# Second layer of a two-layer transformer block: another fill order, the maxima rows of half 0 asked for sooner, the last scaling and stores shared out anew

## The reference

```
x = layernorm(x + attention0(x))      # 16 heads of 8, q and k rms-normed
x = layernorm(x + moe(x))             # top-1 router, 16 experts of 128 -> 512 -> 128, capacity 320
x = layernorm(x + attention1(x))      # 16 heads, d_k 8, d_v 64, causal, then Wo (1024 -> 128)
x = layernorm(x + coupling_ffn(x))    # three cycles of: out += coupling(out) * twist(out)
```

## Time and profile before

| what | value |
|---|---|
| time before, median of 3 runs | 821.2 us (820.27 to 821.78) |
| the profiled execution, its own time | 832.08 us |
| its span (first to last instruction) | 830.4 us |
| PE busy | 775.0 us, 93% of the span |
| DVE / ACT / POOL busy | 63% / 56% / 37% |
| mean granted clock of PE | 0.981 of full speed |

### The profile page before, as it was taken

The page is one execution under the profiler, slowest core; times in us unless marked ns, Lnnn a source line. Parts: engine busy times, 40 slices in busy tenths (PEclk is TensorE's granted clock), DMA queues, the critical chain, the costliest instruction groups (busy, mean ns, idle before and its releaser), DMA issues.

```text
span 830.4 us, 19969 instructions
## 1 busy us (share of the span) xinstructions
PE 775.0 (93%) x7472; PEld 442.4 (53%) x7472; DVE 521.8 (63%) x1400; ACT 464.3 (56%) x737; POOL 311.2 (37%) x466
## 2 busy tenths in 40 slices
PE   6899999999989997899999999999999999999992
PEld 4444444444667776455455555555556555556440
DVE  7488888886511113755766667764776666646556
ACT  3798898899322221364544445543554445554675
POOL 5134433443471004343442345432544323224505
PEclk9799999999999999999999999999999999999997
DMA  6344455433166542315542445414553234222003
GB/s 197 84 114 126 130 136 132 116 103 97 39 147 168 165 124 65 89 50 105 110 85 64 78 103 109 101 38 82 109 110 79 63 65 97 59 59 57 2 1 101
DMA packets 111740, 78.08 MB, mean 94 GB/s; under 512 B 12529, under 2 KB 103089, under 8 KB 111649
## 3 DMA queue, kind: packets, MB, share of 16 engines
q1 hardware_dynamic: 105088, 69.85, 35.1%
q0 software_dynamic: 3664, 5.70, 2.8%
q10 hardware_dynamic: 2896, 1.31, 0.6%
HBM read 37.86 MB, written 13.63 MB: 62 GB/s over the span
## 4 chain that ended last, share of the span: by engine, by line
PE 41%; SPq 12%; DVE 7%; DMA 5%; issue 4%; POOL 2%; ACT 1%; DVEq 0%; POOLq 0%
PE l_ps_v L1473 7%; PE l_ps_c L1446 6%; SPq L113 5%; SPq L115 5%; PE ex_ps_h L1067 5%; PE ex_ps_y L1086 4%; PE l_ps_d L1459 3%; DMA q_ring<-l_max_rows 3%; PE l_ps_v L1374 2%; DVE l_rden L2033 2%; PE l_by_query L1395 2%; DVE l_neg_max L2021 1%; PE l_by_key L1573 1%; PE l_by_query L1386 1%; PE l_by_key L1428 1%
## 5 line engine op out<-in xcount | busy, mean ns | idle before, releaser
L2021 DVE TENSOR_REDUCE l_neg_max<-l_by_query 128x6 bf16<-128x768 f32 x125 | 119.6, 957 | 119.1 <-PE l_by_query L1399 118.8
L2303 POOL TENSOR_SCALAR_AFFINE_SELECT l_probs<-l_probs 128x512 f32<-128x512 f32 x128 | 87.2, 681 | 195.6 <-ACT l_probs L1726 194.7
L1726 ACT ACTIVATE l_probs<-l_by_key 128x768 f32<-128x768 f32 x128 | 103.7, 810 | 69.2 <-PE l_by_key L1431 65.4
L557 ACT ACTIVATE l_probs<-l_ps_s,minus_bound 128x1024 f32<-128x1024 f32 x128 | 137.8, 1122 | 7.7 <-PE l_ps_s L399 5.8
L1446 PE MATMUL l_ps_c<-l_probs,l_values 128*64 128x256 f32 (+1 forms) x1024 | 111.9, 339 | 0.0
L1446 PEld LDWEIGHTS l_ps_c<-l_probs,l_values 128*64 128x64 f32 x1024 | 62.2, 136 | 38.8 <-issue 18.9
L414 PE MATMUL l_ps_o<-l_probs,l_vpad 128*32 128x256 f32 x1024 | 82.0, 393 | 0.2 <-ACT l_probs L557 0.2
L1747 ACT ACTIVATE l_values<-l_ps_v 128x512 f32<-128x512 f32 x63 | 37.6, 597 | 62.8 <-PE l_ps_v L1374 58.9
L1374 PE MATMUL l_ps_v<-w_v,l_xT 128*128 128x512 f32 x126 | 70.8, 644 | 0.0
L1473 PE MATMUL l_ps_v<-w_o,l_ctx 128*128 128x128 f32 x512 | 66.9, 285 | 0.0
L1473 PEld LDWEIGHTS l_ps_v<-w_o,l_ctx 128*128 128x128 f32 x512 | 60.9, 195 | 6.4 <-issue 6.2
(11 more groups left out here) (303 smaller groups left out, 1450.4 us busy)
## 6 DMA issues: line engine op xcount, KB each, us to landing
l_rrep<-rden_d SPq DMA_DIRECT2D x32, 512.0 KB
q_ring<-l_parts SPq DMA_DIRECT2D x192, 64.0 KB
k_ring<-l_parts SPq DMA_DIRECT2D x173, 64.0 KB
w_both<-in_L_ffn_w_dram SPq DMA_DIRECT2D x32, 256.0 KB, 3.3
disp_d<-zeros SPq DMA_DIRECT2D x8, 320.0 KB, 4.1
l_xin<-in_L_attn_x_dram SPq DMA_DIRECT2D x16, 128.0 KB, 2.7
l_xr<-in_L_attn_x_dram SPq DMA_DIRECT2D x16, 128.0 KB, 2.5
x_d<-l_x SPq DMA_DIRECT2D x16, 128.0 KB
```

Source lines behind the costliest of these rows:

```text
L557: act.activation(probs[c % RING][:, :], ps_s[c % 2][:, :], ACT.Exp, bias=k["minus_bound"][:, :], scale=SCALE).then_inc(probs_sb, 1)
L1726: act.activation(probs[c % P_RING][:, :, 0:N + P], by_key[:, :, 0:N + P], ACT.Exp, scale=SCALE).then_inc(p_sb, 1)
L2021: dve.tensor_reduce(neg_max[:, :, half, :, h].rearrange("p a u -> p u a"), query_scores(b, c)[:, :, 0:3 * P].rearrange("p u (a q) -> p u a ...
L2303: pool.affine_select(out=corners, in_=corners, compare_op=ALU.is_ge, fill=0.0, base=0, pattern=[[0, 4], [1, P]], channel_multiplier=-1).th ...
```

## The change

Four edits, all in `second_layer`:

1. Fill. DVE takes `rest` of batch 0 ahead of `second_input(1)`, copies x of batch 1 out of PSUM in place of ACT, and splits batch 1 ahead of the first maxima; POOL fetches batch 3 last; SP loads the queries of batch 1 ahead of the first rows; ACT takes the first maxima rows after the last keys.
2. Steady state. `maxima_by_head(b + 1, 0)` stands ahead of `scores_by_key(b, 6)` and `context(b, 4)` on PE, `maxima_out` ahead of `exponential(b, 6)` on ACT, and the rows of half 0 ahead of the two part-2 loads on SP.
3. The last scaling. In half 0 DVE scales group 1 as well, POOL group 2 instead of 1, ACT only group 3 (in three pieces). In half 1 the inverse roots come as 4 + 4 + 8 columns instead of 4 x 4, and ACT takes 3, 3, 3, 2 blocks of the groups.
4. The last store is two of 128 KB, the first issued by SP, the second by ACT.

```diff
@@ SP
+        def store(eng, g, pieces, piece):
+            n = GB // pieces
+            t = g * GB + (piece - 1) * n
+            eng.wait_ge(normed[g], piece)
+            eng.dma_start(out[t * P:(t + n) * P, :].rearrange("(j p) c -> p j c", p=P), result[:, t:t + n, :]).then_inc(stored, 16)
...
                 load_high_queries(1)
+                load_other_queries(1)
                 rows_to_stack(0, 0)
-                load_other_queries(1)
                 rows_to_stack(0, 1)
...
+                if real(b + 1):
+                    rows_to_stack(b + 1, 0)
+                if real(b + 2):
                     sp.wait_ge(lo_sb, b + 3)
                     load_slots(sp, 2, parts[b % 2], q_ring[i], k_ring[i], stacks_in[i])
                 if real(b + 1):
-                    rows_to_stack(b + 1, 0)
                     rows_to_stack(b + 1, 1)
...
-            for g in range(HALVES * GROUPS):
-                sp.wait_ge(normed[g], 1)
-                sp.dma_start(...)
+            for g in range(HALVES * GROUPS - 1):
+                store(sp, g, 1, 1)
+            store(sp, HALVES * GROUPS - 1, 2, 1)
@@ PE, step
+                maxima_by_head(b + 1, 0)
                 scores_by_key(b, 6)
                 context(b, 4)
-                maxima_by_head(b + 1, 0)
@@ ACT, first_steps
                 load_keys(0, 0)
-                x_out(1)
...
-                maxima_out(0, 0)
                 load_keys(1, 1)
                 load_keys(1, 2)
+                maxima_out(0, 0)
@@ ACT, step
+                maxima_out(b + 1, 0)
                 exponential(b, 6)
-                maxima_out(b + 1, 0)
@@ ACT, end
-            scale_last(0, 2, range(0, 2))
+            scale_last(0, 3, range(0, 2))
             gelu3(RUNS - 1)
-            scale_last(0, 2, range(2, 4))
+            scale_last(0, 3, range(2, 4))
             tanh4(RUNS - 1)
-            scale_last(0, 3, range(GB))
             for g in range(GROUPS):
-                act.wait_ge(factor_step, 4 + 2 * (g + 1))
-                scale_last(1, g, range(ACT_BLOCKS))
+                act.wait_ge(factor_step, 4 + 2 * min(g + 1, 3))
+                scale_last(1, g, range(ACT_BLOCKS[g]))
+            store(act, HALVES * GROUPS - 1, 2, 2)
@@ DVE, first_steps
                 add_expert(1)
+                remainder(0)
                 second_input(1)
-                lower_parts(0)
+                middle_part(0)
+                dve.wait_ge(xT_ps, 2)
+                dve.tensor_copy(xT[1][:, :], ps_m[:, 0:N]).then_inc(xT_sb, 1)
                 add_expert(2)
-                second_input(2)
+                lower_parts(1)
                 for c in range(4):
                     maxima(0, c)
-                lower_parts(1)
+                second_input(2)
@@ DVE, end
             last_factors(0, slice(GB, HB), 2, 2)
+            last_scale(1)
+            last_move(0, 1)
             dve.wait_ge(by_pool, 1)
-            last_move(0, 1)
+            last_move(0, 2)
             couple(5)
             variances(1)
             dve.wait_ge(by_act, 2)
-            last_move(0, 2)
+            last_move(0, 3)
...
+            last_factors(1, slice(0, GB), 3, 4)
+            last_factors(1, slice(GB, 2 * GB), 4, 6)
+            dve.wait_ge(by_act, 3)
+            dve.wait_ge(by_pool, 2)
+            last_move(1, 0)
+            last_factors(1, slice(2 * GB, HB), 5, 8)
+            for g in range(1, GROUPS):
+                dve.wait_ge(by_act, 3 + g)
+                dve.wait_ge(by_pool, 2 + g)
+                last_move(1, g, 1 if g < GROUPS - 1 else 2)
@@ POOL, first_steps
                 root2(1)
-                gather(3)
                 low_part(0)
                 root2(2)
                 low_part(1)
+                gather(3)
@@ POOL, end
-            scale_last(0, 1, range(GB))
-            for g in range(GROUPS):
-                last_root(1, slice(g * GB, (g + 1) * GB))
-                if g > 0:
-                    scale_last(1, g - 1, range(ACT_BLOCKS, GB))
-            scale_last(1, GROUPS - 1, range(ACT_BLOCKS, GB))
+            scale_last(0, 2, range(GB))
+            last_root(1, slice(0, GB))
+            last_root(1, slice(GB, 2 * GB))
+            scale_last(1, 0, range(ACT_BLOCKS[0], GB))
+            last_root(1, slice(2 * GB, HB))
+            for g in range(1, GROUPS):
+                scale_last(1, g, range(ACT_BLOCKS[g], GB))
```

More of the change, by code:

```diff
@@ L1259, in second_layer @@
         CROSSED = 3
-        ACT_BLOCKS = 3
+        ACT_BLOCKS = (3, 3, 3, 2)
         block = ctx.enter_context(nc.Block())
@@ L1337, in _ @@
                 step(b)
-            for g in range(HALVES * GROUPS):
-                sp.wait_ge(normed[g], 1)
-                sp.dma_start(out[g * W:(g + 1) * W, :].rearrange("(j p) c -> p j c", p=P),
-                             result[:, g * GB:(g + 1) * GB, :]).then_inc(stored, 16)
-            sp.wait_ge(stored, 16 * HALVES * GROUPS)
+            for g in range(HALVES * GROUPS - 1):
+                store(sp, g, 1, 1)
+            store(sp, HALVES * GROUPS - 1, 2, 1)
+            sp.wait_ge(stored, 16 * (HALVES * GROUPS + 1))
         @block.tensor
@@ L2040, in divide, with remainder, middle_part @@
                                       rrep[:, :, j, :], ALU.mult).then_inc(divided, 1)
+            def remainder(b):
+                s = split.batch(b)
+                dve.wait_ge(hi_sb, b + 1)
+                at_least(dve, lo_sb, b)
+                s.did(dve.tensor_tensor(rest[:, :], ps_m[:, :], parts[b % 2][:, 0, :], ALU.subtract))
+            def middle_part(b):
+                s = split
+                s.wait()
+                s.did(dve.tensor_copy(parts[b % 2][:, 1, :], rest[:, :]))
+                s.end()
             def lower_parts(b):
                 if real(b):
[L2044 to L2050, removed]
+                    remainder(b)
+                    middle_part(b)
             def first_steps():
@@ L2203, in last_scale @@
             def last_scale(g):
-                dve.wait_ge(factor_step, 2)
+                dve.wait_ge(factor_step, 2 * g + 2)
                 for j in range(GB):
@@ L2209, in last_scale, with last_move @@
                 last.then_inc(by_self, 1)
-                dve.wait_ge(by_self, 1)
-            def last_move(s, g):
+                dve.wait_ge(by_self, g + 1)
+            def last_move(s, g, stored_apart=1):
                 for j in range(GB):
@@ L2216, in last_move @@
                                                     ALU.mult, ALU.add)
-                last.then_inc(normed[s * GROUPS + g], 1)
+                    if (j + 1) % (GB // stored_apart) == 0:
+                        last.then_inc(normed[s * GROUPS + g], 1)
             def last_step():
@@ L2378, in scale_last @@
             def scale_last(s, g, blocks):
-                pool.wait_ge(factor_step, 4 if s == 0 else 4 + 2 * (g + 1))
+                pool.wait_ge(factor_step, 4 if s == 0 else 4 + 2 * min(g + 1, 3))
                 for j in blocks:
```

## The result

The kernel after takes 814.38 us in the median (814.11 to 815.06, 4 runs); beside it the kernel before took 821.49 (820.27 to 824.83, 4 runs). The ratio is 0.9889, 95% interval 0.9860 to 0.9918. The two measures differ: the medians are 7.1 us apart, the ratio stands for 9.1 (6.7 to 11.5). The forecast was 814.3, 6.9 us less than 821.2, in a range of 808.5 to 819.0. On another chip, with 9 runs against 21, the ratio was 0.9931 (0.9900 to 0.9963): the quotient of the medians of the first comparison (0.9913) lies in both intervals.

What follows compares the result with a forecast made beforehand. PE, busy 93%, was taken as the bound, with time won only where it waits. Half of the steady state's 10.2 us, 5.1, plus fill 1.6 and end 0.2 made 6.9 off 821.2: 814.3 us, range 808.5 to 819.

Steps and rivals of the forecast that it cites:

- the waits are jitter that overran a small slack: Steady batches: PE's waits for the maxima rows, behind all 10.9 us of excess, come from varying issues and landings.
- rival (e): Steady batches: PE reaches the transposition about 1.3 us sooner and waits there for `combined`, making the kernel slower; chance 0.07.
- The sum of 10.2: Gain in 13 steady batches of the profiled execution from rows issued sooner: 10.2 us, bounds 8.4 and 10.9.
- The transposition's 0.7: Fill: `rest` of batch 1 done before the maxima no longer delays PE's transposition, 0.7 us won.
- The 0.9 of the first scores: Fill: with the gather last, POOL's `low_part(0)` and then PE's first scores start about 0.9 us sooner.
- What was feared of DVE: Fill: splitting batch 1 before the maxima has 0.5 us of cover; `add_expert(2)` beside `low_part`, 2.29 us before, still overlaps.
- -0.4 for contention: Last scaling: POOL scaling beside DVE makes `couple(5)` 0.4 us late, bounds 0 and 0.7.
- +0.1 for the chain behind the variances: End: three roots fewer win only 0.1 us up to the last move, because ACT's blocks come last.
- +0.5 for the store: Last store: halves of 128 KB land in 1.8 us where 256 KB took 2.3, 0.5 us won.
- Halving edit 2 for plain runs: From profile to median: half of the steady state's 10.2 us, 5.1, was taken to remain in plain runs.
- case (b): Steady batches: all the waits exist in plain runs too, giving 808 to 812 us; chance 0.25.
- (c): Steady batches: few waits exist in plain runs, the gain is the fill and little else, 817 to 819.6 us; chance 0.15.

Runs made afterwards that it cites:

- `fill_only`: The kernel before with the fill edit alone; ratio 0.9967 (0.9945 to 0.9989) to the kernel before, 2.7 us less, median 822.4.
- `steady_only`: The kernel before with the steady-state edit alone (SP's order, PE's transposition, ACT's copy); ratio 0.9915 (0.9886 to 0.9944), 7.0 us less, median 818.57.
- the delayed rows: The kernel before with one or two small loads ahead of the rows on SP; 836.45 us, ratio 1.0061, and 841.19 us, ratio 1.0129.

## Why the prediction was right, point by point

**What bounds it.** Right. Of the 9.8 us won in the profiles from the warm-up on, 8.4 lie in the steady batches, where PE stood idle for the rows. Wrong in part was "the waits are jitter that overran a small slack": the issue alone was past the threshold of 11.9 us in 8 of 13 batches, by SP's queue, and gives 5.1 of the 10.9 us. It gives 5.1 to 5.8 us in all five profiles whose SP order is the old one and has no load added; what is left, late landings, the clock and, in two of them, the 0.11 a batch, is 5.8 us in the kernel before and 1.2 to 3.1 in the other four. So the queue's part is steady, and the profile that the forecast started from had more of the rest than any other.

**Edit 2.** The 1.28 us sooner are 1.31. No wait at the transposition, so rival (e) is out (PE reaches it 1.1 us sooner, 407.42 against 406.36 in the kernel before, not 1.3). The clock stayed at 1.00 in the outlier, the better of the two cases. The sum of 10.2 in the profiled execution came out as 8.4, the lower bound: 1.4 us of the difference are a term that was put at nothing, "PE does the same work": the moves on PE and ACT cost 0.11 a batch. The rest is the late batch, which kept 1.1 us over its floor instead of 0.7.

**Edit 1.** 1.6 forecast, 1.0 from profile to profile, 2.7 (0.9 to 4.5) in plain runs of `fill_only` on one chip; on the two others, where the gap of DVE is, what it brings was not measured by itself, and the fills of the profiles show no gain. The transposition's 0.7 came, where DVE's gap didn't take it back. The 0.9 of the first scores was mis-sized: from the warm-up they begin at 17.46 instead of 17.89 us, 0.43 sooner, though POOL's part is ready 1.1 sooner. The next limit is the queue: SP issues six loads of queries in 4.18 us, one each 0.64 or a little more (timelines of SP and PE):

```profile
322.49 4.18 SPq L113 DMA_DIRECT2D q_ring<-l_parts  x6
...
328.29 0.30 PE L1394 MATMUL l_by_query<-corner,ident_bf 64*64 64x256 bf16 x2 [1.07 <-DMA q_ring<-l_parts]
```

PE still waits 1.07 us there, now for `q_ring` and not for `k_ring`. What was feared of DVE did not come: its split ended 0.70 us before the first maxima could begin, and the two operations of `add_expert(2)`, which began beside POOL's `low_part(0)`, took 1.11 us instead of 2.29.

**Edits 3 and 4.** 0.2 forecast, 0.36 in the profile, nothing that can be measured in plain runs. The forecast was -0.4 for contention, +0.1 for the chain behind the variances and +0.5 for the store; the profiles have -0.04 (`couple(5)` 0.08 us behind tanh, 0.04 before), +0.33 (8.50 us from the variances to the end of the last move before, 8.17 after) and +0.16 (2.78 us from there to the end of the span, then 2.62). All three were mis-sized, and the sum came near by offsetting errors. In the chain the last to end are not ACT's blocks (808.80) but DVE's twelve moves, which run without a pause to 810.28. Contention was too dear (the kernel after, DVE and POOL):

```profile
798.54 2.31 DVE L2232 SCALAR_TENSOR_TENSOR l_values<-l_probs,l_factors,l_values 128x128 f32<-128x128 f32 x8
800.77 0.22 DVE L2159 SCALAR_TENSOR_TENSOR l_coupling<-l_tanh_t,l_spread_t,l_base 128x16 f32<-128x16 f32 x1
...
806.83 3.45 DVE L2232 SCALAR_TENSOR_TENSOR l_values<-l_probs,l_factors,l_values 128x128 f32<-128x128 f32 x12
...
797.41 1.99 POOL L2400 TENSOR_SCALAR l_values<-x,l_factors,l_shift 128x128 f32<-128x128 f32 x4 [0.89 <-DVE l_shift L2217]
```

POOL's four blocks took 1.99 us, not 2.6, and `couple(5)` starts 0.08 us behind tanh (800.42 + 0.27), not 0.4. POOL's four blocks of half 1, beside moves for nearly their whole time, took 2.31 (806.26 on). The Trainium skill's rule on the SBUF lock ("SBUF — State Buffer", section "Who interferes with whom") would have given 2.9; the trace doesn't bear out a full move of 0.29 for each of the four blocks. The blocks began beside a scaling with one input and met the moves only from 798.54 on, and 1.99 - 1.76 = 0.23 is about one move; that only the overlapping part counts is a reading and not shown. The halves of the last store (median us from issue to landing):

```profile
out_dram<-l_values SPq DMA_DIRECT2D x1, 128.0 KB, 2.3
out_dram<-l_values ACTq DMA_DIRECT2D x1, 128.0 KB, 2.2
```

2.2 and 2.3 us are what 256 KB took the earlier trace rows; the 1.8 of `eout_d` was not their price. By the Trainium skill, "DMA: Bandwidth & Descriptors", section "Issuing engines are not separate DMA queues", the halves share the engines; these rows fit that, but don't show it.

**From the profile to the median.** Here the working was weakest, and the figure came out right partly by luck. Halving edit 2 for plain runs gave 5.1; `steady_only` measured 7.0 (4.6 to 9.4), and its profile against those with the old order 335.3 - 329.7 = 5.6. The 5.1 lies inside that interval, so this run alone doesn't refute the halving; the delayed rows do, as far as they go: plain runs lost 5.0 and 10.7 us where the profiles lost 5.3 and 11.2. So plain runs have the waits in about the same measure as the profiles, and case (b)'s mechanism is the likelier one; its 808 to 812 was missed because the 10.2 was too high for a plain run. The first profile had more than its share: 337.2 where two others took 334.9 and 333.7. The sum of the parts was off as well: 7.0 + 2.7 + 0 = 9.7 us on one chip, 5.7 for the whole on another, 9.1 by the ratio and 7.1 by the medians in the first comparison. The forecast of 6.9 meets the last of these to 0.2 us, closer than its terms were.

The 10.9 us by which the profiled execution exceeded the median, equal to the excess of its steady state, led me to (c) and to the halving. That equality said nothing; they lay in good part elsewhere. The warm-up begins at 310.8 to 315.2 us in the profiles taken where the kernel before has a median of 821 to 824, and at 316.5 to 319.9 in those from the chips of 830; 318.57 is in the second group, as its 832.08 us are. ACT's copy of the rows points the same way: in its old place it ends 10.1 us behind the reciprocals in all 13 batches of the three profiles from the chip of 824, and 10.5 to 10.8 in most batches of the four from the chips of 830 and of the kernel before. That the recording of the kernel before came from such a chip is likely, not shown. That 7.7 us of the difference to the profile after are in unchanged stages is shown.

## What to carry to other kernels

A queue that one engine issues in order is a schedule of its own: count the issues ahead of the transfer that the critical engine waits for, at the start-to-start time of each, and look for the offset in the batch beyond which a later issue lengthens the batch one for one. If delaying that transfer on purpose lengthens the plain runs by what the offset says, the waits are real, and moving it the other way pays until it is inside the offset and no further. Before a profiled execution is compared with another or with a median, subtract the stages whose code is the same.

## What the runs showed that I had not expected

The eighth of the 13 batches is longer than its floor in all fourteen profiles: the loads that wait for its reciprocals go out 3.3 to 4.0 us behind them, 1.7 in most other batches. A load of four rows holds SP's queue for 0.43 to 0.54 us, one of a stack 0.64. In the fill the clock fell to 0.50 behind a stretch in which PE was busy 0.85 of 2 us, and stayed at 1.00 in another recording behind 0.27 of 2 us. The new fill seems to gain on one chip and not on two others. The kernel before takes 821 to 830 us in the median, by the chip.
